# Attention block and linear attention in one kernel: a new order of loads and instructions, a fold in two products, one last store

## What is computed

```python
# layer 0: group norm (32 groups), attention over 256 rows, one head
h = group_norm(x, gn_scale, gn_bias)
q, k, v = h @ wq + bq, h @ wk + bk, h @ wv + bv
attn = softmax(q @ k.T * c ** -0.5)
x1 = (attn @ v) @ wo + bo + x
# layer 1: linear attention, 8 heads of 16 channels
q, k, v = split(x1 @ w_qkv + b_qkv)
q = softmax(q, over the 16 channels of a head); k = softmax(k, over the 256 rows)
out = (q @ (k.T @ v per head)) @ w_out + b_out
y = x1 + out * sigmoid(gamma) + beta
```

## Time and profile before

| what | us |
|---|---|
| median of 3 runs | 60.99 (60.9 to 61.57) |
| the profiled execution, its own time | 61.08 |
| span of the profile | 59.0 |

### The profile page before, as it was taken

One profiled execution on the slowest core, in us unless ns is written; L12 is line 12 of the kernel. 1 busy time (PEld: TensorE's weight loads), 2 busy tenths in 40 slices (PEclk: granted clock), 3 DMA queues, 4 the chain that ended last, 5 costly groups with the idle time before them and its releaser, 6 DMA issues.

```text
span 59.0 us, 1435 instructions
## 1 busy us (share of the span) xinstructions
PE 53.8 (91%) x436; PEld 52.5 (89%) x436; DVE 46.3 (78%) x164; ACT 42.8 (72%) x128; POOL 36.9 (63%) x70
## 2 busy tenths in 40 slices
PE   1999999999999999999999999999999999998500
PEld 1998999999999999999999999999999999986400
DVE  1017578999759898898999999889999989998500
ACT  0184265889999999899999778999489997833000
POOL 4881147404998999999981406999913484928000
PEclk9999999999999999999999999999999999999999
DMA  0696765330000000000000000000002020222260
GB/s 0 176 255 158 267 184 67 76 64 11 0 0 6 0 6 0 0 6 11 0 0 0 0 0 0 0 0 0 11 0 89 0 89 0 89 89 89 89 180 3
DMA packets 4712, 2.97 MB, mean 50 GB/s; under 512 B 1249, under 2 KB 4705, under 8 KB 4705
## 3 DMA queue, kind: packets, MB, share of 16 engines
q1 hardware_dynamic: 3984, 2.56, 16.1%
q10 hardware_dynamic: 720, 0.33, 1.9%
HBM read 1.84 MB, written 1.05 MB: 49 GB/s over the span
## 4 chain that ended last, share of the span: by engine, by line
PE 89%; DVE 2%; issue 1%; ACT 1%; DVEq 0%
PE bank L1042 12%; PE bank L991 7%; PE bank L993 7%; PE bank L992 7%; PE bank L930 6%; PE bank L1012 6%; PE bank L1082 6%; PE bank L1097 6%; PE bank L1033 6%; PE bank L937 4%; PE bank L1087 3%; PE bank L1049 3%; PE bank L1075 3%; PE bank L1018 3%; PE bank L1091 3%; PE bank L999 2%
## 5 line engine op out<-in xcount | busy, mean ns | idle before, releaser
L356 POOL TENSOR_TENSOR q<-q,q_max 128x256 f32<-128x256 f32 x8 | 5.0, 620 | 8.1 <-DVE q_max L753 8.1
L1042 PE MATMUL bank<-vals,probsT 128*128 128x129 f32 x64 | 8.5, 276 | 0.0
L1042 PEld LDWEIGHTS bank<-vals,probsT 128*128 128x128 f32 x64 | 7.8, 191 | 0.0
L489 ACT ACTIVATE probs<-bank,neg_smax 128x256 f32<-128x256 f32 x16 | 6.6, 474 | 0.0
L654 DVE BATCH_NORM_STATS2 stats<-bank 128x6 f32<-128x256 f32 x8 | 3.3, 422 | 3.8 <-PE bank L937 3.7
L345 POOL TENSOR_TENSOR hT_lo<-hT,hT_hi 128x256 fp32r<-128x256 f32 x6 | 4.3, 727 | 2.5 <-ACT hT_hi L472 2.5
L361 POOL TENSOR_TENSOR q<-q,q_inv 128x256 f32<-128x256 f32 x8 | 4.9, 624 | 1.5 <-DVE q_inv L761 1.5
L351 POOL TENSOR_TENSOR x_all<-x_all,val_bias 128x256 f32<-128x256 f32 x8 | 5.8, 731 | 0.0
L367 POOL TENSOR_TENSOR y_all<-x,y_bias 128x256 f32<-128x256 f32 x8 | 5.8, 736 | 0.0
L930 PE MATMUL bank<-rest 128*128 128x256 f32 x17 | 4.6, 404 | 1.3 <-DVE rest L784 1.3
L720 DVE TENSOR_REDUCE neg_smax<-bank 128x2 f32<-128x512 f32 x8 | 5.5, 683 | 0.2
(11 more groups left out here) (131 smaller groups left out, 187.3 us busy)
## 6 DMA issues: line engine op xcount, KB each, us to landing
out_y<-y_all SPq DMA_DIRECT2D x7, 128.0 KB, 1.7
x_all<-in_x SPq DMA_DIRECT2D x3, 256.0 KB, 3.9
x_all<-in_x SPq DMA_DIRECT2D x2, 128.0 KB, 2.5
w<-in_L_conv_w_qkv SPq DMA_DIRECT2D x1, 192.0 KB, 5.4
wq_s<-in_L_conv_wq ACTq DMA_DIRECT2D x1, 64.0 KB, 2.7
wk_s<-in_L_conv_wk ACTq DMA_DIRECT2D x1, 64.0 KB, 2.7
wv_s<-in_L_conv_wv ACTq DMA_DIRECT2D x1, 64.0 KB, 3.7
wo_s<-in_L_conv_wo ACTq DMA_DIRECT2D x1, 64.0 KB, 3.5
```

The costliest lines, as they stand in the source:

```text
L356: pool.tensor_tensor(grouped(q[:, b, :]), grouped(q[:, b, :]), over_heads(q_max[:, b, :]), ALU.subtract).then_inc(qsh_ready, 1)
L489: e = act.activation(probs[:, b % RING, j, :], s_ps(b)[:, j, :], ACT.Exp, bias=neg_smax[:, b, j:j + 1])
L1042: m = pe.matmul(att_ps[:, j, :], probsT[:, b % RING, k, j * P:(j + 1) * P], vals[:, b, k, :], start=(k == 0), stop=(k == J - 1))
```

## The change

Nothing is computed otherwise. These things differ:

- POOL_H takes batches 1 and 3 as well, so `h_norm_pool` makes h of 1 and 3 to 7, and VectorE that of 0 and 2.
- PSUM banks are given out anew.
- SyncE's queue: x of 0, 1, gn_scale, x of 2 and 3, of 4 and 5, of 6 and 7, then wv and wo, then as before. ScalarE's queue: wq, wk, then the columns gn_bias, bq, bv.
- The product of gn_bias with wq and that with wv are two steps with banks, semaphores and VectorE copies of their own (`q_bias_product`, `v_bias_product`, `fold_copy`, `fold_v_copy`).
- The last batch is stored whole by SyncE, when both halves are there; half 0 is made first; ScalarE has no store.
- The lists of steps of GpSimd, ScalarE, VectorE and TensorE have a new order. `turn_over` passes are 10, 1, 4, 5, 1, 2 and 2 where they were 10, 1, 4, 1 and 1.

The diff, cut: of the long lists the head and, where it matters, the end.

```diff
     STAT_SETS = [(0, 1), (1, 2), (2, 4), (4, 8)]
     PLAIN_U = (0, 1)
     PLAIN_K = ()
-    POOL_H = (4, 5, 6, 7)
+    POOL_H = (1, 3, 4, 5, 6, 7)
     RING = 4
-    XT_BANKS, S_BANKS = (0, 1, 5, 6), (0, 1, 3)
+    XT_BANKS, S_BANKS = (3, 4, 2, 5), (0, 4, 2)
     BANK = {
-        "wT": 5, "fold": 2, "a_bias": 3, "a": 0, "wvT": 3, "wvo": 1, "stats": 7, "y_bias": 0,
-        "val_bias": 4, "u": 2, "val": 3, "att": 5, "x1T": 6, "kT": 7, "qT": 6, "k": 4,
-        "x1k": 0, "ctx": 2, "m": 3, "y": 1, "last_y0": 4, "last_y1": 7,
+        "wT": 1, "fold": 1, "fold_v": 0, "a_bias": 6, "a": 3, "wvT": 6, "wvo": 7, "stats": 7,
+        "y_bias": 5, "val_bias": 6, "u": 1, "val": 3, "att": 5, "x1T": 6, "kT": 7, "qT": 2,
...
             load_x(0)
             load_x(1)
+            sp.dma_start(vec[:, GNS:GNS + 1], column(gn_scale)).then_inc(scale_in, 16)
             load_x(2)
-            sp.dma_start(vec[:, GNS:GNS + 1], column(gn_scale)).then_inc(scale_in, 16)
-            for n, v in ((GNB, gn_bias), (BQ, bq), (BV, bv)):
-                sp.dma_start(vec[:, n:n + 1], column(v)).then_inc(columns_in, 16)
             load_x(3)
             load_x(4)
+            sp.dma_start(wv_s[:, :], wv).then_inc(wv_in, 16)
+            sp.dma_start(wo_s[:, :], wo).then_inc(wo_in, 16)
             sp.dma_start(bo_b[:, :], every_row(bo)).then_inc(bo_in, 16)
             sp.dma_start(w1[:, :, :], w_qkv.rearrange("k (a c) -> k a c", a=3)).then_inc(w1_in, 16)
             sp.dma_start(gamma_b[:, :], every_row(flat(gamma))).then_inc(gamma_in, 16)
@@ -259,9 +261,10 @@
             for b in range(B - 1):
                 after(sp, y_ready, b)
                 sp.dma_start(y_d[b], y_all[:, b, :]).then_inc(stored, 16)
-            sp.wait_ge(half_y_ready[1], 1)
-            sp.dma_start(last_half(y_d[B - 1], 1), last_half(y_all[:, B - 1, :], 1)).then_inc(stored, 16)
-            sp.wait_ge(stored, 16 * (B + 1))
+            for j in range(J):
+                sp.wait_ge(half_y_ready[j], 1)
+            sp.dma_start(y_d[B - 1], y_all[:, B - 1, :]).then_inc(stored, 16)
+            sp.wait_ge(stored, 16 * B)
 
         @block.gpsimd
         def _(pool):
@@ -301,7 +304,7 @@
                 return pool.tensor_copy(out[:, :], column.to_broadcast([P, C]))
 
             def v_bias_rows():
-                pool.wait_ge(fold_ready, 1)
+                pool.wait_ge(fold_v_ready, 1)
...
 
             constants()
             set_rstd(0)
+            set_rstd(1)
+            h_norm_pool(1)
+            set_rstd(2)
             v_bias_rows()
-            set_rstd(1)
+            h_norm_pool(3)
             a_low()
-            set_rstd(2)
             h_low(2)
             h_low(3)
+            w1_low()
+            set_rstd(3)
+            x_plus_bias(0)
+            h_norm_pool(4)
             sigmoid_plus()
-            x_plus_bias(0)
-            set_rstd(3)
             x_plus_bias(1)
...
-            q_normal(1)
+            q_shift(4)
             q_normal(2)
-            x1_plus_bias(2)
+            q_normal(3)
             x1_plus_bias(3)
+            q_shift(5)
             x1_plus_bias(4)
-            q_normal(3)
...
             weight_loads()
             qk_copy()
             xT_copy(0)
-            wv_copy()
             xT_copy(1)
+            a_copy()
             xT_copy(2)
-            wvo_copy()
-            a_copy()
-            xT_copy(3)
             a_high()
             a_bias_copy()
+            xT_copy(3)
             u_copy(0)
-            val_copy(0)
+            wv_copy()
             xT_copy(4)
             xT_copy(5)
-            xT_copy(6)
+            wvo_copy()
             u_copy(1)
             h_high(2)
-            val_copy(1)
+            w1_high()
+            val_copy(0)
+            gamma_exp()
             s_exp(0)
             h_high(3)
-            gamma_exp()
...
             m_copy(6)
             m_copy(7)
-            act.wait_ge(half_y_ready[0], 1)
-            act.dma_start(last_half(y_d[B - 1], 0), last_half(y_all[:, B - 1, :], 0)).then_inc(stored, 16)
 
...
             def fold_copy():
                 dve.wait_ge(fold_done, 1)
-                dve.tensor_tensor(fold[:, :], fold_ps, vec[:, BQ:BV + 1], ALU.add).then_inc(fold_ready, 1)
+                dve.tensor_tensor(fold[:, 0:1], fold_ps, vec[:, BQ:BQ + 1], ALU.add).then_inc(fold_ready, 1)
+
+            def fold_v_copy():
+                dve.wait_ge(fold_v_done, 1)
+                dve.tensor_tensor(fold[:, 1:2], fold_v_ps, vec[:, BV:BV + 1], ALU.add).then_inc(fold_v_ready, 1)
 
...
             dve.memset(rest[:, :].bitcast(F32), 0.0).then_inc(rest_set, 1)
             channel_stats(0)
             set_means(0)
-            channel_stats(1)
             set_neg_means(0)
             set_variances_own(0)
+            channel_stats(1)
             set_means(1)
+            set_variances(0)
             channel_stats(2)
-            set_variances(0)
+            set_variances_own(1)
+            set_neg_means(1)
             channel_stats(3)
-            set_neg_means(1)
-            set_variances_own(1)
-            fold_copy()
             set_scales(0)
             set_means(2)
             set_variances(1)
+            fold_copy()
             h_norm(0)
             set_variances_own(2)
+            set_scales(1)
             set_neg_means(2)
-            set_scales(1)
             channel_stats(4)
-            h_norm(1)
+            channel_stats(5)
             set_variances(2)
-            channel_stats(5)
             channel_stats(6)
+            fold_v_copy()
+            channel_stats(7)
             set_scales(2)
-            channel_stats(7)
             h_norm(2)
             s_max(0)
...
             q_sums(7)
             y_rows(4)
+            q_turn_back(6)
+            q_recip(7)
             ctx_mask(7)
-            q_recip(7)
-            q_turn_back(6)
+            k_recip(7)
             y_rows(5)
-            k_recip(7)
             q_turn_back(7)
             y_rows(6)
+            y_half_rows(0)
             y_half_rows(1)
-            y_half_rows(0)
 
...
-            def bias_products():
+            def q_bias_product():
                 pe.wait_ge(columns_in, 16 * 3)
+                pe.matmul(fold_ps, wq_s[:, :], vec[:, GNB:GNB + 1], start=True, stop=True).then_inc(fold_done, 1)
+
+            def v_bias_product():
                 pe.wait_ge(wv_in, 16)
-                pe.matmul(fold_ps[:, 0:1], wq_s[:, :], vec[:, GNB:GNB + 1], start=True, stop=True)
-                pe.matmul(fold_ps[:, 1:2], wv_s[:, :], vec[:, GNB:GNB + 1], start=True, stop=True).then_inc(fold_done, 1)
+                pe.matmul(fold_v_ps, wv_s[:, :], vec[:, GNB:GNB + 1], start=True, stop=True).then_inc(fold_v_done, 1)
 
...
             pe.wait_ge(rest_set, 1)
-            turn_over(10, 0)
+            turn_over(10, 3)
             pe.wait_ge(ident_ready, 1)
             x_transposes(0)
+            turn_over(1, 4)
             x_transposes(1)
+            turn_over(4, 7)
+            means(0)
             qk_transposes()
-            turn_over(1, 7)
-            means(0)
-            pe.wait_ge(wT_copied, 1)
-            turn_over(4, 5)
+            variances(0)
+            turn_over(5, 2)
             x_transposes(2)
-            x_transposes(3)
-            variances(0)
-            wv_transpose()
-            pe.wait_ge(xT_copied, 1)
-            a_product()
             pe.wait_ge(var_ready, 1)
             turn_over(1, 7)
             means(1)
-            bias_products()
-            pe.wait_ge(xT_copied, 2)
-            wvo_product()
+            x_transposes(3)
+            pe.wait_ge(xT_copied, 1)
+            a_product()
             variances(1)
-            a_bias_product()
-            turn_over(1, 4)
-            val_bias_product()
-            pe.wait_ge(var_ready, 2)
-            means(2)
+            turn_over(2, 1)
+            q_bias_product()
             pe.wait_ge(a_full_ready, 1)
             x_transposes(4)
+            pe.wait_ge(var_ready, 2)
+            turn_over(2, 7)
+            means(2)
+            a_bias_product()
+            x_transposes(5)
             u_plain(0)
+            pe.wait_ge(xT_copied, 3)
+            x_transposes(6)
+            variances(2)
+            v_bias_product()
             pe.wait_ge(a_bias_ready, 1)
-            val_product(0)
-            variances(2)
-            x_transposes(5)
-            x_transposes(6)
+            wv_transpose()
+            pe.wait_ge(xT_copied, 4)
+            x_transposes(7)
             pe.wait_ge(u_hi_ready, 1)
             u_plain(1)
-            x_transposes(7)
-            pe.wait_ge(xT_copied, 5)
+            pe.wait_ge(var_ready, 3)
+            wvo_product()
+            pe.wait_ge(fold_v_ready, 1)
             s_plain(0)
+            val_product(0)
+            s_plain(1)
+            u_product(2)
+            means(3)
+            pe.wait_ge(val_ready, 1)
             val_product(1)
-            s_plain(1)
+            p_transposes(0)
```

(39 more changed lines are left out.)

391 lines of the change are left out of this document (182 added, 209 removed).

## The result

The changed kernel takes 62.28 us (median of 4 runs, 61.97 to 62.51); in the same comparison the kernel before took 61.28 (4 runs, 60.90 to 61.62). The ratio is 1.018, 95% interval 1.0123 to 1.0237: slower, and above the range of the prediction. A ratio leaves out executions that took over 1.5% longer than the quickest of the same kernel, so it can differ from the quotient of two medians. The profiled execution of the changed kernel took 61.97 us by its own time, with a span of 59.9.

What follows compares the result with a forecast made beforehand. TensorE's instruction list was taken to bound the kernel from about 5.9 to 52 us. 61.08 + 0.6 + 0.2 + 0.1 - 1.0 = 61.0 us, 60.9 on the median's scale; range 60.1 to 62.1.

Steps and rivals of the forecast that it cites:

- The body: Kernel ahead of the final stores, set by TensorE's instruction list: forecast 0.9 us slower.
- the end: Landing of the last store: forecast 1.0 us faster.
- The last store: Whole store on SyncE lands after 1.7 us, not 2.8, if the instruction fetch misses it: -1.0 us, bounds -1.1 and 0.1.
- Rival B: At the last store's landing: no gain if an instruction fetch again falls just behind the last issue; 61.9 us, chance 0.25.
- h on GpSimd: h of batches 1 and 3 moved off VectorE: GpSimd has room, VectorE's relief worth nothing; 0, bounds -0.1 and +0.8 us.
- turn_over: TensorE's early passes, 25 instead of 17: five more at the fast level, 0.12 each; +0.6 us, bounds 0 to +1.0.
- Rival C: Extra passes free through an earlier TensorE level change, ladder at the end shorter, end gains: 60.1 us, chance 0.17.
- Loads: Reordered DMA queues: later columns, wv, wo hidden, x of 4 to 7 not awaited before; 0 us.
- qk_transposes: Two TensorE instructions moved from the slow into the fast stretch, 0.11 each: +0.2 us, bounds 0 to 0.2.
- small waits: TensorE waits at variances(0) for var_t and p_transposes(0) for s_exp(0): +0.1 us, bounds 0 and +0.4.
- Statistics: Early statistics chain, checking whether TensorE waits: forecast means(0) end near 5.95, var_g(0) 6.85, h_norm(0) 8.95, u_plain(0) 9.6 us.
- Rival D: GpSimd or ScalarE late between 12 and 20 us, making TensorE wait 0.8 to 1 us: 62.2 us, chance 0.13.

Runs made afterwards that it cites:

- b_whole: Kernel before with the last batch stored whole by SyncE instead of as two halves; 61.51 us, ratio 1.005.
- b_hpool_whole: Kernel before with h of batches 1 and 3 on GpSimd and the last batch stored whole by SyncE; 59.93 us, ratio 0.9792.
- b_h3: Kernel before with only h of batch 3 moved to GpSimd; 59.67 us, ratio 0.976.
- b_hpool: Kernel before with h of batches 1 and 3 moved to GpSimd, nothing else; 59.76 us, ratio 0.9773.
- b_hpool_dve4: Kernel before with h of batches 1 and 3 on GpSimd, plus four one-column memsets at the start of VectorE's list; 60.51 us, ratio 0.9836.
- a_few: Changed kernel with 17 turn_over passes instead of 25; 60.83 us, ratio to the kernel before 0.9858.
- b_more: Kernel before with eight more turn_over passes, 25 in all; 61.89 us, ratio 1.0115.
- the repeated pair: Changed kernel with 17 turn_over passes, measured again with new and with old DMA queue orders, 11 runs each; 61.28 and 60.96 us.
- a_few_oldloads: Changed kernel with 17 turn_over passes and both DMA queues in their old order; 60.75 us, ratio to the kernel before 0.986.
- b_few: Kernel before with only the first ten turn_over passes, seven removed; 63.80 us, ratio 1.0269.
- a_hdve: Changed kernel with h of batches 1 and 3 back on VectorE; 62.72 us, ratio 1.0268.
- a_few_dve4: Changed kernel with 17 turn_over passes, plus four one-column memsets at the start on VectorE; 64.87 us, no ratio.
- a_few_again: Changed kernel with 17 turn_over passes, measured again on another chip, 11 runs; 61.28 us, ratio 0.998.
- a_wide: Changed kernel with turn_over passes paired to 512 columns, TensorE's list 22 instructions shorter; 61.71 us, ratio 1.017.
- a_oldloads: Changed kernel with 25 turn_over passes and both DMA queues in their old order; 62.43 us, no ratio.

## Why the prediction was wrong

On the profiled executions' own time the sum was 61.0 and the measurement 61.97. The body was forecast at +0.9 and came at +1.17 (0.27 of the miss), the end at -1.0 and came at -0.28 (0.72 of it). The median lies 0.3 above the profiled execution, which was the quickest of four.

- **The last store, -1.0: this step failed.** Its picture of the kernel before was right: one landing is held up beside an instruction fetch, and the form of the store does not matter (b_whole, b_hpool_whole). The claim that VectorE's shorter list moves that fetch off was right too, as b_h3, b_hpool and b_hpool_dve4 show. What failed is "I take the case that it misses the last store": a second fetch, on q8, fell on the same place, and the end gained 0.28 us instead of 1.0. It did not hold one landing up: SyncE's issue took 1.03 us instead of 0.35, and with that 0.7 us the end comes to the 5.95 of a_few. I treated as one event what are several lists with fetches of their own, and the change had touched all the lists. Rival B had the place and 61.9, with a fetch behind the last issue; this one began 0.3 us ahead of it. After was profiled once, so whether its other three executions have the packet there is not known. The rule of the Trainium skill (Trainium Kernel Development and Optimization, Key Constraints), that issuing from several engines only saves issue time, is borne out by b_whole, where SyncE's whole store took 2.73 us.
- **h on GpSimd, 0: priced wrongly.** Its own stretch was read correctly: GpSimd had room, and y6 moved by only 0.18 us in the order of before. But the edit shortens VectorE's list, and that is 1.0 us of tail in the order of before. I had named the effect under the last store and given it no edit.
- **turn_over, +0.6.** +0.61 in b_more, +0.83 with the old loads, +0.17 with the new ones. The size was about right for passes on a busy TensorE, but the count behind it was not. The level was misread: in the kernel before it comes near 5.1 us, with 11 of the 17 passes ahead of it, and in the changed one near 4.1, with 11 of the 25, so 8 passes more ran at the upper level and not 5. Rival C had named an earlier level, but its reason is not borne out: the four passes begin at 4.29, behind the change, and b_more has the level at 4.3 with the head of before. By C's rule of half the time the 1.0 us gave back 0.5 at most, so without it the body would have lost up to 1.7 us (an estimate: 1.17 + 0.5).
- **Loads, 0: failed.** That x of 4 to 7 "is not awaited before" is true and beside the point: I had not followed x of 2 and 3, which is issued 0.47 us later behind gn_scale and lands 1.1 us later. It cost 0.71 us in a_few by y6, a part of which is the later level there (0.3 by the medians of the repeated pair, not clear of noise), and nothing more beside the five passes, which fill the wait for it.
- **The new order.** a_few_oldloads has y6 at 54.47, b_hpool, with as many passes, the old loads and the same h, at 54.00, though its level comes 0.6 us later. So the new lists themselves cost some 0.5 us by these two executions; which of their moves does it was not tried one by one. The qk_transposes (+0.2) and the small waits (+0.1) are in this sum and were not measured apart.
- **Statistics.** means(0) was forecast to end near 5.95, and neg_mean, which follows it, started at 5.39; var_g(0) was forecast at 6.85 and came at 6.15; h_norm(0) at 8.95 and came at 8.90; u_plain(0) at 9.6 and came at 9.89; u_plain(1) at 10.9 and came at 11.27; y_product(6) at 55.1 and came at 55.35.
- **Rival D** is excluded: TensorE is busy 39.99 of 40.00 us from 12 to 52.

## What to carry to other kernels

An instruction fetch shows among the DMA packets: look for packets of kind "instruction" beside the last store, and compare their time with its landing, before giving the store a new form. A step moved from one engine to another changes the length of two lists, and at the end of a kernel that can be worth more than the step itself (here 1.0 against 0.2 us). Where a list has filler passes, test an edit with and without them: fillers hide a late load (here the five passes), and in b_few, without seven of them, the upper level came 8 us later.

## What was not expected of the hardware

- The last store lands about 1 us later when one 8 KB instruction packet runs beside it: 1.8 against 2.7 to 2.9 us for ScalarE's half, 1.75 against 2.73 for a whole batch (2.4 in a_hdve and a_few_dve4). The packet itself takes only 0.3 to 0.6 us. With 192 or 193 records in VectorE's list it came 2.3 to 3.3 us behind y6 in all seven profiles, which is beside the store; with 188 to 190 it came 5.0 to 6.2 us behind y6, which is after the landing.
- Beside the 16 KB packet an issue on SyncE took 1.03 us instead of 0.35. That is one case, and no rule: in a_few_again an issue at 45.18 us stands inside a 16 KB packet (44.11 to 45.58) and took 0.34.
- Some executions took 63 to 66 us, beside those of b_few: with 17 passes in the new order 5 of 11 with the new loads (a_few_again) and 1 of 11 with the old, 4 of 5 in a_few_dve4, 3 of 11 in a_wide, 1 of 5 in a_hdve and 1 of 4 in a_oldloads; the kernel before had one such too, 66.37 us. The only profile of one in the new order is a_few_dve4's, with the granted clock back at 0.50 for 6.8 us, which makes a mean of 0.946. Three of the five long ones of a_few_again have a mean of 0.945, which fits that; the other two (65.72 and 65.83) and the one with the old loads have 1.0, and their cause is not known.
- What calls for the q8 packet stays open: a_wide, with a shorter TensorE list, lost it from the end, but so did a_oldloads and a_hdve, with an unchanged one. a_oldloads has a median 1.1 us above its profiled execution, which would fit a packet that falls now on the store and now behind it; no second profile was taken of it.
